# Causal attention with a gated mixture of experts on one core: mask and row maximum in one VectorE instruction that writes negated scores

## What is computed

```python
xn = _layernorm(x, axis=-1)
q = xn @ WQ; k = xn @ WK; v = xn @ WV
scores = einsum('bsd,btd->bst', q, k) / sqrt(dk)
scores = where(causal, scores, -inf)
attention = softmax(scores, axis=-1)
s = einsum('bst,btd->bsd', attention, v)
g = silu(ffn(xn))          # router with top 2 of 8 experts, and a shared expert
out = x + s * g
```

## Time and profile before

| | us |
|---|---|
| median of 3 runs (lowest to highest) | 238.85 (238.68 to 239.2) |
| the profiled execution | 240.62 |
| its span | 238.6 |
| PE busy, share of the span | 230.6, 97% |
| DVE busy | 186.8, 78% |
| ACT busy | 144.9, 61% |
| POOL busy | 55.4, 23% |

### The profile page before, as it was taken

How to read it: one execution, slowest core, us unless ns; L and a number is a source line. 1 busy time by engine, 2 the same in 40 slices (tenths; PEclk the granted TensorE clock), 3 DMA queues, 4 the chain that set the end, 5 groups by cost and what they waited for, 6 DMA issues and landing times.

```text
span 238.6 us, 4677 instructions
## 1 busy us (share of the span) xinstructions
PE 230.6 (97%) x1533; PEld 205.8 (86%) x1533; DVE 186.8 (78%) x620; ACT 144.9 (61%) x392; POOL 55.4 (23%) x108
## 2 busy tenths in 40 slices
PE   7898999999999999999999999999999999999983
PEld 5788998998989989999899998898988889898843
DVE  3779859989899899897977985677776867869765
ACT  2444745755648457474574723779678696878722
POOL 5220631805509136073012000002020201202000
PEclk9999999999999999999999979999999999999999
DMA  5699420020200200000000000116847557393523
GB/s 156 207 326 304 157 91 1 1 87 5 88 3 0 88 3 3 0 3 0 0 3 1 0 3 0 48 26 196 142 105 197 76 145 122 103 199 57 140 74 102
DMA packets 18758, 19.45 MB, mean 82 GB/s; under 512 B 1064, under 2 KB 17712, under 8 KB 18736
## 3 DMA queue, kind: packets, MB, share of 16 engines
q1 hardware_dynamic: 15568, 16.02, 21.4%
q0 software_dynamic: 3168, 3.15, 9.1%
HBM read 14.95 MB, written 4.21 MB: 80 GB/s over the span
## 4 chain that ended last, share of the span: by engine, by line
PE 92%; DMA 2%; DVE 2%; ACT 1%; issue 1%; SPq 1%; DVEq 0%; ACTq 0%
PE bank L392 85%; PE bank L484 4%; PE bank L440 3%; DMA raw_qkv<-in_L_attn_WK 2%; DVE raw_sw L1382 1%; DVE w L1380 1%; PE bank L556 1%; PE bank L414 0%; SPq L220 0%; DVE arena L949 0%; ACT xT_hi_all L731 0%; ACT arena L731 0%; ACT probs L731 0%; ACT attn_all L731 0%; SPq L222 0%
## 5 line engine op out<-in xcount | busy, mean ns | idle before, releaser
L392 PE MATMUL bank<-xT_hi_all,arena 128*128 128x512 f32 (+3 forms) x256 | 80.7, 370 | 0.7 <-DVE arena L949 0.7
L392 PE MATMUL bank<-arena 128*128 128x256 f32 (+2 forms) x560 | 76.8, 285 | 0.3 <-ACT attn_all L731 0.3
L392 PEld LDWEIGHTS bank<-arena 128*128 128x128 f32 (+1 forms) x560 | 71.9, 186 | 5.0 <-issue 0.8
L392 PEld LDWEIGHTS bank<-xT_hi_all,arena 128*128 128x128 f32 x256 | 47.0, 189 | 8.3 <-ACT probs L761 1.4
L731 ACT ACTIVATE arena<-bank 128x512 fp32r<-128x512 f32 (+4 forms) x84 | 36.2, 452 | 24.4 <-PE bank L392 23.1
L949 DVE TENSOR_TENSOR arena<-bank,arena 128x264 fp32r<-128x264 f32 (+4 forms) x83 | 41.4, 508 | 6.9 <-ACT arena L731 6.0
L392 PE MATMUL bank<-xT_lo_all,arena 128*128 128x512 f32 (+3 forms) x128 | 45.8, 358 | 0.0
L383 POOL DMA_DIRECT2D x_ring<-in_L_attn_x x6 | 7.9, 1317 | 79.0 <-DVE x_ring L1318 79.0
L392 PEld LDWEIGHTS bank<-xT_lo_all,arena 128*128 128x128 f32 x128 | 24.2, 189 | 2.1
L731 ACT ACTIVATE attn_all<-bank,row_inv 128x256 f32<-128x256 f32 x32 | 15.2, 474 | 17.3 <-PE bank L392 15.5
L761 ACT ACTIVATE probs<-bank,neg_max 128x128 f32<-128x128 f32 (+3 forms) x32 | 17.0, 530 | 12.6 <-DVE neg_max L1008 12.5
(11 more groups left out here) (128 smaller groups left out, 381.9 us busy)
## 6 DMA issues: line engine op xcount, KB each, us to landing
x_ring<-in_L_attn_x SPq DMA_DIRECT2D x7, 512.0 KB, 3.5
x_ring<-in_L_attn_x POOLq DMA_DIRECT2D x6, 512.0 KB, 6.0
out<-x_ring SPq DMA_DIRECT2D x6, 512.0 KB, 3.3
spread<-pairs SPq DMA_DIRECT2D x14, 128.0 KB, 3.3
w_sb<-in_L_ffn_w SPq DMA_DIRECT2D x1, 1024.0 KB, 11.9
raw_sw<-in_L_ffn_sw SPq DMA_DIRECT2D x3, 256.0 KB, 4.2
x_ring<-in_L_attn_x SPq DMA_DIRECT2D x2, 256.0 KB, 2.9
xn<-in_L_attn_x SPq DMA_DIRECT2D x1, 512.0 KB, 5.3
```

The costliest lines, as they stand in the source:

```text
L392: return nc.tensor.matmul(dst, lhsT, rhs, start=start, stop=stop, skip_group_check=True, **kw)
```

## The change

The mask becomes `causal_wide`, 512 columns: zeros, with the triangular mask in the last 128. For a row of n columns its last n columns are used, so that the triangle lies on the diagonal block. One instruction adds it to the whole row, multiplies by -1, writes this back over the scores and keeps the minimum of what it wrote, which is the negated maximum. The exponential reads negated scores and so scales by -1. The semaphore `masked` goes. `zero_bf` and `causal_bf` become parts of the wide tile, so POOL has one memset less, and a longer one.

```diff
-        causal_bf = sb("causal_bf", [P, P], BF16)
-        zero_bf = sb("zero_bf", [P, D], BF16)
+        causal_wide = sb("causal_wide", [P, S], BF16)
+        causal_bf = causal_wide[:, S - P:S]
+        zero_bf = causal_wide[:, 0:D]
...
-            made(nc.gpsimd.memset(causal_bf[:, :], 0.0))
+            made(nc.gpsimd.memset(causal_wide[:, :], 0.0))
...
-            made(nc.gpsimd.memset(zero_bf[:, :], 0.0))
...
-            pool.wait_ge(s["const_part"], 7)
+            pool.wait_ge(s["const_part"], 6)
...
-            pe.wait_ge(s["const_part"], 7)
+            pe.wait_ge(s["const_part"], 6)
...
-                nc.scalar.activation(probs[:, i % 2, 0:n], sc_bank[i % 2][:, 0:n], ACT.Exp, bias=neg_max[:, i:i + 1],
+                nc.scalar.activation(probs[:, i % 2, 0:n], sc_bank[i % 2][:, 0:n], ACT.Exp, bias=neg_max[:, i:i + 1], scale=-1.0,
...
             def row_max(b, i):
                 dve.wait_ge(s["scores_done"], T * b + i + 1)
-                last = sc_bank[i % 2][:, i * P:(i + 1) * P]
-                nc.vector.tensor_tensor(last, last, causal_bf[:, :], ALU.add).then_inc(s["masked"], 1)
-                dve.wait_ge(s["masked"], T * b + i + 1)
-                nc.vector.tensor_reduce(neg_max[:, i:i + 1], sc_bank[i % 2][:, 0:(i + 1) * P], AX.X, ALU.max,
-                                        negate=True).then_inc(s["max_done"], 1)
+                n = (i + 1) * P
+                row = sc_bank[i % 2][:, 0:n]
+                nc.vector.tensor_tensor_reduce(out=row, in0=row, in1=causal_wide[:, S - n:S], scale=-1.0, scalar=-MASKED,
+                                               op0=ALU.add, op1=ALU.min, accum_out=neg_max[:, i:i + 1]).then_inc(s["max_done"], 1)
```

More of the change, by code:

```diff
@@ L189, in build @@
             stats_part stats_done rstd_part rstd_done centered xn0_tiles xn_done x_turned x_hi x_lo
-            v_summed v_hi v_lo logits_kept q_summed q_hi q_lo scores_done masked max_done exp_done
+            v_summed v_hi v_lo logits_kept q_summed q_hi q_lo scores_done max_done exp_done
             p_turned pT_hi pT_lo pv_done inv_done attn_kept
@@ L299, in _ @@
                                          pattern=[[1, G], [-1, G]], channel_multiplier=0))
-            pool.wait_ge(s["const_part"], 10)
+            pool.wait_ge(s["const_part"], 9)
             nc.gpsimd.tensor_copy(ident_bf[:, :], ident[:, :]).then_inc(s["const_ready"], 1)
```

## The result

The changed kernel takes 237.39 us (median of 20 runs, 236.92 to 240.39), the kernel before 239.11 us (20 runs, 238.32 to 240.19). The ratio is 0.9943, with a 95% interval of 0.9921 to 0.9965: 1.36 us less, between 0.8 and 1.9. The prediction had 1.28. The medians lie 1.72 apart, more than the ratio says, because the ratio is one of means: four of the changed kernel's 20 runs show a mean granted clock of 0.985 or 0.993 and take 238.74 to 240.39 us. The other sixteen (clock 0.996 or more) have a median of 237.30.

The account below looks back on a forecast made before the run. PE was taken as the bound, waiting for exponentials behind DVE's row maximum. Rounds 1 to 5 0.90, round 6 0.11, round 0 0.10 and b = 7 0.17 sum to 1.28 us: 238.85 to 237.6 us, range 236.8 to 239.1.

Parts of the forecast that it names:

- What bounds the kernel: PE is the bound, busy 92% of the span; DVE matters only through seven weight-load waits for the exponential.
- What a stall costs: At PE's weight load before `scores`, 0.24 us idle costs the matmul stream only 0.18 us per round.
- The sum that can be won: All stalls behind the exponential, rounds 0 to 6 and b = 7, together hold 1.34 us at most.
- The pass: The fused DVE instruction costs what the reduce cost, 0.42 us at 256 columns; at most 66 ns more at 128.
- The accumulator read: Added on DVE after the pass: 0.15 us, between 0.08 and 0.19; a tile then gains 0.17 us.
- DVE's busy time: DVE gets some 0.6 us per round back, some 5 us less busy in all.
- Tile 1 starts earlier: Tile 0's gain lets tile 1's work on DVE start at 66.92 in place of 67.02, 0.10 us earlier.
- At no cost: The exponential's scale of -1 and POOL's one longer memset, about 0.54 us where two took 0.53, cost nothing.
- rival 4: Pass and read dearer than mask and reduce: seven rounds lose about 0.7 us, or 3 us or more; chance 0.10.
- rival 5: PE's clock fall at 140 to 142 us goes away, 235.9 us, or comes a second time, 239.3; chance 0.05.

Follow-up runs that it names:

- six reciprocals: Changed kernel with six one-column reciprocals on DVE between the wait for the scores and the pass of tile 1: ratio 0.9978 to the kernel before, median 238.31 us.
- three reciprocals: Changed kernel with three one-column reciprocals on DVE between the wait for the scores and the pass of tile 1: ratio 0.9893 to the kernel before.
- The two kernels without the 0.35 us wait: Changed kernel with the last sequence's tile 1 output copy before tile 3's probability copy: 236.80 us; the same plus an unused 8-column tile: 236.18 us.

## Why the prediction was right

The mechanism was right: the waits that it named went, by the path that it named. That its 1.28 lies within 0.1 of the 1.36 of the ratio is in part luck, since the same two kernels differ by 1.43 in the stretches of the mechanism and by 1.72 in the medians. The 0.3 us between the stretches and the medians is not placed.

*What bounds the kernel.* Right. PE is the bound, and its waits for the exponential, with the 0.10 us in round 0 that the list of waits does not show, are the way in which DVE's row maximum reached it. The runs with tiles 0 and 1, tiles 2 and 3, and tile 1 alone share them out between tile 1 and tile 0.

*What a stall costs.* Right: 0.18 us for 0.24 idle. Rounds fell by 0.19 (15.44 to 15.25), and with six reciprocals the wait of 0.27 costs 0.19 again. The sum that can be won was put at 1.34, with no more to be had; the three stretches gave 1.43. Rounds 0 to 5 gave 1.06 for 1.00, round 6 0.13 for 0.11, and b = 7 0.24 for 0.23.

*The pass.* Right: 433 ns at 256 columns and 298 at 128, where the nearest rows had 417 and 281 and the reduce itself 424 and 291. These are the groups of the changed kernel by form:

```profile
L1007 DVE CUSTOM_DVE_ANT_0 bank<-bank,causal_wide 128x512 f32<-128x512 f32 x8 | 5.5, 690 | 0.0
L1007 DVE DVE_READ_ACCUMULATOR2_ANT neg_max<- 128x1 f32 x32 | 4.5, 142 | 0.0
...
L1007 DVE CUSTOM_DVE_ANT_0 bank<-bank,causal_wide 128x256 f32<-128x256 f32 x8 | 3.5, 433 | 1.6 <-PE bank L392 0.9
L1007 DVE CUSTOM_DVE_ANT_0 bank<-bank,causal_wide 128x128 f32<-128x128 f32 x8 | 2.4, 298 | 6.1 <-PE bank L392 6.1
```

*The accumulator read.* The term that was mis-sized. I took 0.15 us on the way and measured 0.06. Its length, 142 ns, was right, but it lies under the end of the pass, as the lower bound from ACT's pair had it. The reason that I gave for 0.15, that DVE starts an instruction before the last has ended, spoke for the lower bound: 0.15 is a read without any overlap. A tile so gained 0.25 to 0.27 us in place of 0.17, a little above the upper end of the range given, 0.24. For tile 1 this changed nothing, since 0.18 was all that PE had lost; for tile 0 of b = 7 it brought 0.24 in place of 0.17. The sentence of the Trainium skill that the prediction names (VectorE: DVE Perf Modes, The DRAIN you can't avoid) would make it a whole read, and the read starts 0.08 us before the pass has ended. But the same section adds: "A next op that is not held starts earlier", and these rows agree with that. The page's advice against fusing for speed does not fit the 0.25 us per tile.

*DVE's busy time.* It fell by 10.2 us and not by 5. The masks' 9.3 went, the pass took the place of the reduce (15.8 after 15.7), and the 32 reads, 4.5 us, run for the most part beside the pass and the next instruction, so they add less than I had counted. Another 2.6 us came from a router step that the change does not touch. These are its groups before and after:

```profile
L1066 DVE SCALAR_TENSOR_TENSOR raw_qkv<-raw_qkv,iota_e 128x32 f32<-128x32 f32 x16 | 5.5, 346 | 0.1
```

```profile
L1065 DVE SCALAR_TENSOR_TENSOR raw_qkv<-raw_qkv,iota_e 128x32 f32<-128x32 f32 x16 | 2.9, 184 | 0.1
```

Before, some of these sixteen instructions last up to 0.70 us, with a median of 0.19; after, none lasts more than 0.19. What stretched them was not tried. No time on PE hangs on it: the kernel with tile 1 alone has the short rounds with 308 ns here.

*Tile 1 starts earlier.* Right, 0.10 predicted; it starts 1.20 us behind `turn_x` in place of 1.31. But it wasn't needed in rounds 1 to 6: with tile 1 alone in the new form they are as short, and only round 0 keeps 0.04 us.

*At no cost.* Right for the memsets, by the kernel with the wide tile alone. For the scale no run stands alone, but the exponential's rows are 0.37 and 0.47 us, after 0.37 and 0.48.

*The rivals.* A pair dearer than mask and reduce (rival 4) was not met. The reciprocals bear on its price: a delay of 0.39 us in front of the measured pair brings the rounds back to those of before, at 0.19 each. That further delay would go on to cost its full length, as the rival says, was not run. The clock (rival 5) rested on a wrong premise. I took the fall at 140 us for part of every run, so that 1.7 us could still be won by losing it. It is in the profiled executions of before, after, and three reciprocals, and in none of the other eleven; the kernel with the wide tile alone has none and took 238.71 us, where the kernel before with the fall took 240.62. Cut at the chain's pieces, the fall costs 1.5 us between 132.5 us and the end of the long piece. That is the larger part of the 1.8 us between the profiled execution and the median, which the prediction noted and did not explain. The median of 238.85 had no fall to lose, and the 235.9 of this rival was out of reach by that way. Since both profiled executions happened to have the fall, it drops out of their difference. What brings it on is not settled. The two kernels without the 0.35 us wait ahead of it had no fall in their profiles, but nor had most kernels with the wait. By the mean granted clock of each run, none of their 12 runs is below 0.996, against 42 of the 197 runs of the other kernels, that of before among them, for which a clock is on record. At the others' rate, 12 runs without any would come about once in eighteen times: a hint that the wait matters, and too few runs to settle it.

## What to carry to other kernels

When one engine is the bound, look for the waits that it has for the engine that you speed up, and price each by what its stream lost, not by the idle time beside it. Here 10 us less work on VectorE was worth 1.4 us, through seven listed waits and 0.10 us in round 0, and fusing tiles that nobody waits for was worth nothing. Once such a wait is gone the slack behind it can be measured by putting small instructions back until the time moves. And a profiled execution that lies far from the median of its runs has something in it that the others lack; find it before building a sum on that trace. The same holds for a ratio of means over few runs: look at the clock of each run before two ratios are compared.

## What the hardware showed that I had not expected

- The fused pass costs what a reduce of the same width costs, though it reads a second operand and writes the row back (433 and 424 ns at 256 columns, 690 and 692 at 512), and the read of the accumulator shares its start with the next instruction (65.08 and 65.08).
- A shift of the tiles by 32 bytes made PE's long piece of the second half 0.57 us shorter (84.22 to 83.65), a shift by 64 bytes only 0.1, but that one took 0.25 us off the first half. Which of the tiles does it, and why, was not tried.
- The granted clock falls to half, 1.2 GHz, near 140 us in 3 of the 14 profiled executions shown here, the code being the same or nearly so, and costs 1.5 us each time. The mean granted clock of the single runs has two steps: at 0.992 or 0.993 the changed kernel takes about 1.5 us more than at full clock, at 0.985 about 3 us more. Where in the run the clock fell is on record for the profiled executions only.
